# Weighting the one-hot instead of the gathered rows in the two relational passes of a graph network

## The reference

```python
def _rgcn_layer(x, src, dst, edge_type, w_rel, root, bias):
    seg = dst * NUM_REL + edge_type
    xs = x[src]
    sums = segment_sum(xs, seg, N * NUM_REL)
    cnt = segment_sum(ones, seg, N * NUM_REL)
    mean = (sums / maximum(cnt, 1.0)).reshape(N, NUM_REL, -1)
    return einsum('nrd,rdo->no', mean, w_rel) + x @ root + bias

h = maximum(layernorm(x), 0)
x = x + rgcn(relu(rgcn(h, w_rel1)), w_rel2)       # L0
h = maximum(layernorm(x), 0)
x = x + attention(h, src, dst)                     # L1
```

## Time and profile before

| | us |
|---|---|
| median of 3 runs | 12709.82 |
| lowest and highest | 12708.29, 12718.36 |
| the profiled execution | 12666.73 |
| its span, first to last instruction | 12664.9 |
| GpSimd busy in it | 9039.3 (71%) |
| TensorE busy | 7165.4 (57%) |
| VectorE busy | 5372.7 (42%) |
| ScalarE busy | 4183.5 (33%) |

### The profile page before, as it was taken

The page is one execution under the profiler, slowest core; times in us unless marked ns, Lnnn a source line. Parts: engine busy times, 40 slices in busy tenths (PEclk is TensorE's granted clock), DMA queues, the critical chain, the costliest instruction groups (busy, mean ns, idle before and its releaser), DMA issues. The chain is left out here.

```text
span 12664.9 us, 190403 instructions
## 1 busy us (share of the span) xinstructions
PE 7165.4 (57%) x34895; PEld 5988.6 (47%) x34896; DVE 5372.7 (42%) x11674; ACT 4183.5 (33%) x12473; POOL 9039.3 (71%) x9581
## 2 busy tenths in 40 slices
PE   3734444444444864444444444556777777777777
PEld 1333333333333543333333333445666666666666
DVE  7832222222222641111111111453766766666667
ACT  2522222222222222222222222224444444444442
POOL 0167777777777767777777777767777777777776
PEclk8855555555555975555555555667989999989898
DMA  8611111111112531111111111236888888888887
GB/s 246 207 52 52 53 52 53 52 53 52 53 52 64 187 130 52 53 52 53 52 53 52 53 52 53 75 86 179 236 233 233 237 235 235 235 234 237 233 236 212
DMA packets 922698, 1589.79 MB, mean 126 GB/s; under 512 B 303128, under 2 KB 487318, under 8 KB 915334
## 3 DMA queue, kind: packets, MB, share of 16 engines
q0 software_dynamic: 314112, 685.63, 20.1%
q1 hardware_dynamic: 384568, 595.99, 15.1%
q10 hardware_dynamic: 223412, 301.41, 8.0%
HBM read 1213.18 MB, written 367.39 MB: 125 GB/s over the span
## 5 line engine op out<-in xcount | busy, mean ns | idle before, releaser
L714 POOL DMA_INDIRECT p_g<-ytab,p_i x6250 | 5903.3, 945 | 1971.2 <-issue 1631.1
L1165 POOL DMA_INDIRECT a_g<-xlw,a_i x3125 | 2992.3, 958 | 996.4 <-issue 887.3
L678 PE MATMUL p_pg<-p_v,p_oh 128*128 x6120 | 1343.7, 398 | 1550.4 <-ACT p_v L761 1548.7
L761 ACT ACTIVATE p_v<-p_g,wgt_all 128x128 f32<-128x128 f32 x6250 | 1960.4, 389 | 543.2 <-issue 523.2
L678 PEld LDWEIGHTS p_pg<-p_v,p_oh 128*128 128x128 f32 x6120 | 1203.8, 296 | 1711.3 <-issue 1701.5
L755 ACT ACTIVATE p_i<-rel_all 128x5 int32 (+1 forms) x1250 | 260.1, 208 | 5053.6 <-DMA p_g<-ytab,p_i 5053.6
L678 PE MATMUL p_pt<-p_v,p_oh 128*128 x4200 | 979.8, 417 | 1269.3 <-ACT p_v L761 1269.3
L678 PEld LDWEIGHTS p_pt<-p_v,p_oh 128*128 128x128 f32 x4200 | 877.7, 313 | 1368.3 <-issue 1368.3
L1628 PE MATMUL a_px<-a_g,ident 128*128 x1450 | 736.6, 593 | 849.4 <-SPq L1216 741.2
L616 DVE TENSOR_TENSOR p_oh<-p_cols,local 128x640 f32<-128x640 f32 x1460 | 1195.4, 819 | 24.9
L1264 ACT ACTIVATE a_away<-a_dst,a_minus 128x640 f32 x727 | 602.2, 828 | 1386.7 <-issue 843.5
(11 more groups left out here) (254 smaller groups left out, 9807.6 us busy)
## 6 DMA issues: line engine op xcount, KB each, us to landing
a_xj<-xjw ACTq DMA_DIRECT2D x725, 330.0 KB
xjw<-a_g SPq DMA_DIRECT2D x625, 330.0 KB
a_dst<-in_dst_dram SPq DMA_DIRECT2D x625, 320.0 KB
p_g<-ytab,p_i POOLq DMA_INDIRECT x6250
ytab<-steps POOLq DMA_DIRECT2D x98, 640.0 KB, 3.5
ytab<-src_i SPq DMA_DIRECT2D x98, 640.0 KB
ea<-in_edge_attr_dram SPq DMA_DIRECT2D x50, 1176.0 KB
a_g<-xlw,a_i POOLq DMA_INDIRECT x3125
```

The costliest lines, as they stand in the source:

```text
L678: last = t.matmul(pg[b][:, 0:width], onehot[(at + k) % LOOK][:, q * P:(q + 1) * P], V[:, ds(to + q * width, width)], start=(q == 0), stop= ...
L714: pool.indirect_dma_start(gbuf[k][:, q * D:(q + 1) * D], None, rows, bass.IndirectOffsetOnAxis(ap=stage[k][:, q:q + 1], axis=0)).then_inc( ...
L761: last = a.activation(V[:, c:c + D], gbuf[k][:, q * D:(q + 1) * D], ACT.Copy, scale=wgt[:, ds(G * g + q, 1)])
L1165: pool.indirect_dma_start(gbuf[k][:, q * W:(q + 1) * W], None, xlw, bass.IndirectOffsetOnAxis(ap=stage[k][:, q:q + 1], axis=0)).then_inc(s ...
```

## The change

In the relational passes the weights are applied on the other operand of the product.

- VectorE multiplies each one-hot, in place and after the compare, by the weights of the step's five edge tiles (`wgt`, in SBUF, one number an edge over 128 columns). The column number is therefore loaded in p2 too. The multiply waits for the compare through `s_eq` and counts in `s_oh`.
- ScalarE no longer scales. It waits for the landing of group g and for TensorE's end of group g-10, copies the indices of group g+5, and this copy counts in `s_v`. Its loop body is one round.
- The gathers land in `V` itself, a ring of 15 groups that TensorE reads. `gbuf` is gone. GpSimd's loop body is three rounds, with three rounds ahead of it and two behind.
- The tables of the ring are made for 15 places.

```diff
-VSLOTS = 10
+VSLOTS = 15
@@ sum_engines, match
+                    dcol, = load(dve, DVE_, steps, s + PLANE, 1, TILES - G)
                     if localise:
-                        dcol, = load(dve, DVE_, steps, s + PLANE, 1, TILES - G)
...
                     v.tensor_tensor(onehot[k][:, :].rearrange("p (t n) -> p t n", t=G),
                                     colsp[:, 0:P].rearrange("p (a n) -> p a n", a=1).to_broadcast([P, G, P]),
                                     here.rearrange("p (t a) -> p t a", a=1).to_broadcast([P, G, P]),
-                                    ALU.is_equal).then_inc(s_oh, 1)
+                                    ALU.is_equal).then_inc(s_eq, 1)
+                    dve.wait_ge(s_eq, s + 2)
+                    v.tensor_tensor(onehot[k][:, :].rearrange("p (t n) -> p t n", t=G),
+                                    onehot[k][:, :].rearrange("p (t n) -> p t n", t=G),
+                                    wgt[:, ds(dcol, G)].rearrange("p (t a) -> p t a", a=1).to_broadcast([P, G, P]),
+                                    ALU.mult).then_inc(s_oh, 1)
@@ gather_engine
-                def round_(i, peel):
+                parts = VSLOTS // SLOTS
+                def round_(i, part, peel):
...
                         for q in range(G):
+                            c = ((part * SLOTS + k) * G + q) * D
                             pool.indirect_dma_start(
-                                gbuf[k][:, q * D:(q + 1) * D], None, rows,
+                                gbuf[:, c:c + D], None, rows,
                                 bass.IndirectOffsetOnAxis(ap=stage[k][:, q:q + 1], axis=0)).then_inc(s_g[k], 16)
-                round_(0, True)
-                with pool.Fori(1, ROUNDS) as i:
-                    round_(i, False)
+                for i in range(parts):
+                    round_(i, i, i == 0)
+                with pool.Fori(1, ROUNDS // parts) as j:
+                    for part in range(parts):
+                        round_(parts * j + part, part, False)
+                for i in range(ROUNDS // parts * parts, ROUNDS):
+                    round_(i, i % parts, False)
@@ rgcn_pass, scalar
                                 gate(act, "act", (s_g[k], 16 * G * (i + 1)))
-                                a.activation(stage[k][:, :], rel_i[:, ds(G * g + G * SLOTS, G)], ACT.Copy)
                                 if not peel:
-                                    upto, = load(act, ACT_, done, g - VSLOTS, 1, STEPS)
+                                    upto, = load(act, ACT_, done, g - (VSLOTS - SLOTS), 1, STEPS)
                                     gate(act, "act", (s_pe, count(upto)))
-                                for q in range(G):
-                                    c = ((part * SLOTS + k) * G + q) * D
-                                    last = a.activation(V[:, c:c + D], gbuf[k][:, q * D:(q + 1) * D], ACT.Copy,
-                                                        scale=wgt[:, ds(G * g + q, 1)])
-                                last.then_inc(s_v, 1)
+                                a.activation(stage[k][:, :], rel_i[:, ds(G * g + G * SLOTS, G)], ACT.Copy).then_inc(s_v, 1)
```

More of the change, by code:

```diff
@@ L84 @@
 assert all(BLOCK * (NBLK - 2) + OUT_AT[b] >= GROUPS + OB * b + OB - 1 for b in range(OUTS))
+assert VSLOTS % SLOTS == 0 and ROUNDS % (VSLOTS // SLOTS) == 2
 assert AHEAD == UNROLL and NT % 2 == 0 and STEPS + UNROLL <= SCOLS * P
@@ L598, in sum_engines @@
             s_dl, s_oh = sem(f"{name}_local"), sem(f"{name}_onehot")
-            s_cp = sem(f"{name}_cols_set")
+            s_eq = sem(f"{name}_compared")
             @block.vector
@@ L639, in body @@
                             tiles.dve_after(dve, i, k)
-                v.tensor_copy(colsp[:, 0:P], cols[:, :]).then_inc(s_cp, 1)
-                dve.wait_ge(s_cp, 1)
+                v.tensor_copy(colsp[:, 0:P], cols[:, :]).then_inc(s_eq, 1)
+                dve.wait_ge(s_eq, 1)
                 for s in range(LOOK):
@@ L698, in _, with gather_engine @@
                         then.pe(pe, i, k)
-        def gather_engine(block, rows, stage, gbuf, s_stage, s_g, s_free, s_kept=None):
+        def gather_engine(block, rows, stage, gbuf, s_stage, s_g, s_free):
             @block.gpsimd
             def _(pool):
-                def round_(i, peel):
+                parts = VSLOTS // SLOTS
+                def round_(i, part, peel):
                     for k in range(SLOTS):
@@ L710, in round_ @@
                             gate(pool, "pool", (s_free, SLOTS * (i - 1) + k + 1))
-                            if s_kept is not None:
-                                gate(pool, "pool", (s_kept[k], 16 * i))
                         for q in range(G):
+                            c = ((part * SLOTS + k) * G + q) * D
                             pool.indirect_dma_start(
-                                gbuf[k][:, q * D:(q + 1) * D], None, rows,
+                                gbuf[:, c:c + D], None, rows,
                                 bass.IndirectOffsetOnAxis(ap=stage[k][:, q:q + 1], axis=0)).then_inc(s_g[k], 16)
-                round_(0, True)
-                with pool.Fori(1, ROUNDS) as i:
-                    round_(i, False)
+                for i in range(parts):
[5 more added lines that the diff above has]
+                    round_(i, i % parts, False)
         def rgcn_pass(name, first, table, following):
             with ExitStack() as st:
-                gbuf = [sbuf(st, f"{name}_g{k}", [P, G * D]) for k in range(SLOTS)]
                 stage = [sbuf(st, f"{name}_i{k}", [P, G], I32) for k in range(SLOTS)]
@@ L736, in rgcn_pass @@
                 with nc.Block() as block:
-                    gather_engine(block, table.rearrange("n (r d) -> (n r) d", d=D), stage, gbuf, s_stage, s_g, s_v)
+                    gather_engine(block, table.rearrange("n (r d) -> (n r) d", d=D), stage, V, s_stage, s_g, s_v)
                     sum_engines(block, name, onehot, colsp, pg, V, D, s_v, s_pe, s_acc, then, localise=first)
@@ L748, in _, with round_ @@
                             a.activation(stage[k][:, :], rel_i[:, k * G:(k + 1) * G], ACT.Copy).then_inc(s_stage, 1)
-                        def round_(i, part, peel):
+                        def round_(i, peel):
                             for k in range(SLOTS):
@@ L753, in round_ @@
                                 gate(act, "act", (s_g[k], 16 * G * (i + 1)))
-                                a.activation(stage[k][:, :], rel_i[:, ds(G * g + G * SLOTS, G)], ACT.Copy)
                                 if not peel:
-                                    upto, = load(act, ACT_, done, g - VSLOTS, 1, STEPS)
+                                    upto, = load(act, ACT_, done, g - (VSLOTS - SLOTS), 1, STEPS)
                                     gate(act, "act", (s_pe, count(upto)))
-                                for q in range(G):
-                                    c = ((part * SLOTS + k) * G + q) * D
-                                    last = a.activation(V[:, c:c + D], gbuf[k][:, q * D:(q + 1) * D], ACT.Copy,
-                                                        scale=wgt[:, ds(G * g + q, 1)])
-                                last.then_inc(s_v, 1)
[L764 to L771, removed]
+                                a.activation(stage[k][:, :], rel_i[:, ds(G * g + G * SLOTS, G)], ACT.Copy).then_inc(s_v, 1)
+                        for i in range(VSLOTS // SLOTS - 1):
+                            round_(i, True)
+                        with act.Fori(VSLOTS // SLOTS - 1, ROUNDS) as i:
+                            round_(i, False)
         def tile_of(i, k, lag):
```

## The result

| | before | after |
|---|---|---|
| median of 4 runs, us | 12709.06 | 12840.19 |
| lowest and highest | 12702.46, 12718.36 | 12831.43, 12850.85 |
| profiled execution | 12666.73 | 12850.85 |

The ratio is 1.0104 [1.0092, 1.0116]: slower by 131 us. The forecast was 12,784 (slower, +74 us), with a range up to 12,970. The direction and the mechanism held; the price was nearly double the forecast. 12,840 also lies 10 us above the 12,745 to 12,830 that the prediction gave to its forecast alone: only the wide range, made for rivals one and four, takes it in.

What follows compares the result with a forecast made beforehand. GpSimd's gathers, one each 1.249 us, were taken to bound the passes. Regular steps 0, irregular and last-stretch steps +71 and ends +3 gave +74 us: 12,741 profiled, 12,784 in the median; range 12,725 to 12,970.

Steps and rivals of the forecast that it cites:

- Rival one: In the passes, likeliest pass 2, regular steps' multiplies stretch gathers too: 160 us beside the 74, 12,945 us; chance 0.21.
- Rival four: In the last 500 us of pass 1 VectorE becomes the bound: 38 us beside the 74, 12,822 us; chance 0.07.
- GpSimd's beat bounds the passes: In both relational passes, one gather each 1.249 us sets the pace: 7806 us of the 12,665.
- freed ScalarE gains nothing: In the passes, removing 6250 scalings, 1960 us busy on ScalarE, frees nothing by itself.
- A gather is stretched when it starts under a multiply with two SBUF inputs: In the passes, such a gather lasts longer until about 0.13 us before the instruction's end, counted over its own 0.945.
- Rival two: In the passes, the relational gathers are not touched by the multiply; only +3 us remains, 12,713 us; chance 0.13.
- The sum: Over the whole kernel: +71 us for irregular and last-stretch steps and +3 for the ends, +74 us.
- the even phase that I assumed: For 377 irregular and last-stretch steps, multiplies fall evenly over the gathers' beat: 0.188 us each, 71 us.
- I take zero for them: Regular steps of both passes: multiplies start 0.42 and 0.20 us behind a gather's start and stretch none, 0 us.
- The signs: In the passes: gathers of 0.945 us, some 200 long ones up to 1.62, mean 0.957, few among regular steps.
- The ends: Last steps of each pass: 0 us in pass 1, 2.4 in pass 2, taken as +3 together.
- Rival three: GpSimd's 894 waits that end by a scaling, 272.4 us, are real and vanish: 12,438 us; chance 0.04.

Runs made afterwards that it cites:

- no_multiply_2: The changed kernel without the multiply by the weights, run again on another chip than no_multiply; ratio 1.0000 to the kernel before.
- the PSUM run: The changed kernel with the step's weights first copied to PSUM and read there by the multiply; 12,697.49 us against 12,692.34 before, ratio 1.0004.
- early_load_2: The changed kernel with ScalarE's register load and wait for TensorE put ahead of its wait for the landing; 12,977.32 us, ratio 1.0228 to the kernel before.

## Why the prediction was right, and where its size was not

**GpSimd's beat bounds the passes; freed ScalarE gains nothing.** Right. Shown by no_multiply_2, ratio 1.0000.

**A gather is stretched when it starts under a multiply with two SBUF inputs.** Right but for the first 0.045 us, shown by the PSUM run. The inference of the Trainium skill (SBUF — State Buffer, "Who interferes with whom"), by which descriptor generation is not held up by such an instruction, does not hold for these indirect gathers: 1.597 us instead of 0.944. Rival two falls with it.

**The sum.** Each stretched gather of the changed kernel was put to the multiply above it, and the steps sorted as the prediction sorts them (regular: the first step behind its own staging copy, at no more than about 0.3 us from its usual distance to it):

| | steps | stretched | us | forecast us |
|---|---|---|---|---|
| pass 1, before 4050 us, regular | 498 | 333 | 34.3 | 0 |
| pass 2, before 7980 us, regular | 489 | 68 | 31.6 | 0 |
| both, irregular | 238 | 114 | 38.6 | 34 |
| last stretch of each pass, all | 231 | 129 | 46.4 | 37 |

The irregular steps and the last stretches came out close to the even phase that I assumed: 85 us against 71. **The step that failed is "I take zero for them", said of the regular steps**: they cost 66 us (77 if every first step behind a copy is counted as regular). It has two causes.

*Phase, pass 1.* Where no gather has been stretched since the group's last one, the multiply starts 0.67 us behind a gather's start and not 0.42, beyond the 0.56 at which stretching begins; over all regular steps the median is 0.61. The terms, as medians over the middle of the passes: load and wait ahead of the staging copy 0.58 us, not 0.43; compare to multiply 0.95, not 0.86 (the wait on a long instruction is 0.13, not the 0.04 of a short one); 0.44 from copy to TensorE as forecast. The two errors add up to 0.24, and 0.42 + 0.24 = 0.66. In pass 2 the two terms are 0.59 and 0.96, add to compare is 0.60 and not 0.69, and the compare of before stood 0.47 behind a gather's start in the median, not 0.43 as in the one step that I read: 0.20 + 0.16 + 0.10 - 0.09 + 0.04 = 0.41, and 0.43 was measured. There it did no harm by itself. The negative feedback showed too: 333 steps by only 0.10 us.

*Knock-on, pass 2.* A phase of 0.43 is free, and yet 68 regular steps were hit, by 0.46 us each. In 62 of them a gather had already been stretched between the group's last gather and the multiply. The steps that were not hit give the comparison: of about 100 regular steps with such a stretch behind them 62 were hit, of 390 without one only 6. That stretch moves the beat back by up to 0.65 us while the chain keeps its time, so the multiply lands just ahead of the next start, stretches that one too, and so on. The timeline of pass 2, three regular steps behind an irregular one:

```profile
5218.32 0.83 DVE L622 TENSOR_TENSOR p_oh<-p_oh,wgt_all 128x640 f32<-128x640 f32 x1
...
5218.48 1.49 POOL L721 DMA_INDIRECT p_v<-ytab,p_i  x1 [0.30 <-issue]
...
5222.49 0.82 DVE L622 TENSOR_TENSOR p_oh<-p_oh,wgt_all 128x640 f32<-128x640 f32 x1
5222.76 1.37 POOL L721 DMA_INDIRECT p_v<-ytab,p_i  x1 [0.30 <-issue]
...
5229.37 0.82 DVE L622 TENSOR_TENSOR p_oh<-p_oh,wgt_all 128x640 f32<-128x640 f32 x1
5229.43 1.59 POOL L721 DMA_INDIRECT p_v<-ytab,p_i  x1 [0.30 <-issue]
...
5236.02 0.82 DVE L622 TENSOR_TENSOR p_oh<-p_oh,wgt_all 128x640 f32<-128x640 f32 x1
5236.31 1.35 POOL L721 DMA_INDIRECT p_v<-ytab,p_i  x1 [0.30 <-issue]
```

I had written that a stretch moves the beat and took this for a brake alone. It is a brake for a phase above the edge and a push for one below it. The same explains the miss of early_load_2 in pass 1: at a phase of 0.13 us three of 346 regular steps were hit on their own, and over 100 with a stretch behind them, of about 120 (some 40 us). This reading rests on sorting the rows of two kernels; no run was made that takes the irregular steps away.

**The signs.** Of those that the prediction named, the usual gather of 0.945 us, the tail up to 1.6 and the long gathers under the multiply came out. Some 200 long gathers and a mean of 0.957 did not (644 and 0.968), and neither did "few among regular steps": 401 of the 644. That the total stayed inside the range is in part luck, since nothing in the prediction bounded the knock-on.

**The ends.** +3 us were expected; with the multiply from PSUM or left out the whole is +5 and -5 us against before, within what can be told.

**Rival one** (a regular step falls over the edge, likeliest in pass 2) happened in part: by its phase in pass 1, and in pass 2 nearly always by knock-on. It cost 66 us and not 160: in pass 1 the steps lie just over the edge, and in pass 2 few were hit. **Rival three** is out: GpSimd's idle time stayed at 1971 us when the scalings went; it is now booked as "issue". **Rival four** is not needed: the last 510 us of pass 1 hold 395 gathers at 0.987 us (389.91/395) of GpSimd, VectorE busy at 68% (344 of 510). With 0.30 us of idle time each the gathers fill 508 of the 510 us.

## What to carry to other kernels

When GpSimd's descriptor making is the bound, price a new VectorE instruction first by what it reads from SBUF and only then by its length: with one of its two inputs in PSUM the multiply was free, with both in SBUF it cost 131 us. Counting inputs is not enough, as the tensor_scalar above shows; look in the trace at hand for gathers that start under an instruction of the same kind. A stretch can be sized from the trace of before: the end of the two-input instruction minus the gather's start minus 0.13 us. Where the two engines are locked to one another, work out the phase with each wait measured in its own place, and follow what a first collision does to the next multiply before taking a free phase for safe.

## What the runs showed of the hardware

- A gather of 0.944 us that starts under the multiply with two SBUF inputs is longer by what is left of the multiply, minus 0.127 us. One that starts before the multiply or in its first 0.045 us is not touched (in the second case the multiply takes up to 0.90 us). With one operand in PSUM no gather is stretched.
- A tensor_scalar from SBUF to SBUF with one tensor input stretched all seven gathers of the trace of before that start under it; a tensor_reduce of one SBUF tensor leaves 356 of 358 alone.
- The wait on one's own engine cost 0.04 us behind a 0.16 us instruction and 0.13 us behind a 0.82 us one, start of the next minus end of the first.
- On one chip the kernel before took 15,559 us and not 12,709. In the trace of no_multiply from that chip 732 matmuls in 3000 us stand behind waits of 1.6 to 3.3 us for which the profile shows no cause; the same kernel's trace from another chip has none. The three kernels without the scalings took 0.8 to 1.4% less there than the kernel before (no_multiply 0.986), the one that keeps them did not (1.001).
